# Four graph layers in one kernel: another place for the messages, squares as rows of the distance product, and new orders of the first two slots and of the last two graphs

## The reference

```
x = _layernorm(x + _L0(x, adj))
x = _layernorm(x + _L1(x, adj))
x = _layernorm(x + _L2(x, adj))
x = _layernorm(x + _L3(x, adj, nodemask))

# _L0: message passing with a gated state
h = relu(bn1(conv1(x.T)));  h = bn2(conv2(h, 17 taps));  x_conv = relu(h + x.T).T
s = x @ w_se.T + b_se                      # three columns
sq = sum(s * s, -1)
A = exp(-(sq[:, None] + sq[None, :] - 2 * s @ s.T)) * adj
x_nmp = A @ relu(x @ w_msg.T + b_msg)
r, z, n = gates of (x_conv, x_nmp, x);     return (1 - z) * n + z * x
# _L1: attention
X, q, k = leaky(x @ W_lin + b), leaky(x @ W_q), leaky(x @ W_k)
A = adj * sigmoid(q @ k.T * scale);  d = sum(A, -1) ** -0.5;  return (d * A * d) @ X
# _L2: hyperbolic aggregation
t = artanh(|x|) * x / |x|;  u = adj @ t;  return project(tanh(|u|) * u / |u|)
# _L3: normalised adjacency with its own loops
A = adj + I;  d = (sum(A, -1) + eps) ** -0.5;  return relu((d * A * d) @ (x @ W + b) * mask)
```

## Time and profile before

| what | us |
|---|---|
| median of the three runs shown | 773.96 |
| the profiled execution's own time | 773.77 |
| its span in the profile | 772.0 |
| PE busy | 709.7 (92%) |
| DVE busy | 625.5 (81%) |
| ACT busy | 423.6 (55%) |
| POOL busy | 138.0 (18%) |

### The profile page before, as it was taken

One profiled execution on the slowest core, in us unless ns is written; L12 is line 12 of the kernel. 1 busy time (PEld: TensorE's weight loads), 2 busy tenths in 40 slices (PEclk: granted clock), 3 DMA queues, 4 the chain that ended last, 5 costly groups with the idle time before them and its releaser, 6 DMA issues.

```text
span 772.0 us, 12824 instructions
## 1 busy us (share of the span) xinstructions
PE 709.7 (92%) x3984; PEld 547.4 (71%) x3984; DVE 625.5 (81%) x2080; ACT 423.6 (55%) x881; POOL 138.0 (18%) x151
## 2 busy tenths in 40 slices
PE   3879999999999999999999999999999999998553
PEld 1757877777787867777787867778687777775531
DVE  7456788888888888888888888888888888876655
ACT  4153754747374665748375665738465565734431
POOL 0000121221121111122121111112121121111221
PEclk9999999999999999999999999999999999998886
DMA  5304333150614233160513234060523324101000
GB/s 204 123 0 134 113 110 110 65 182 14 207 39 149 82 122 122 34 211 14 183 62 128 103 110 135 16 228 14 177 68 119 112 81 164 56 15 55 5 10 28
DMA packets 46585, 75.33 MB, mean 98 GB/s; under 512 B 4064, under 2 KB 12768, under 8 KB 46432
## 3 DMA queue, kind: packets, MB, share of 16 engines
q1 hardware_dynamic: 46560, 75.02, 28.9%
HBM read 70.82 MB, written 4.19 MB: 97 GB/s over the span
## 4 chain that ended last, share of the span: by engine, by line
PE 81%; ACT 10%; DVE 5%; issue 3%; POOL 1%; DMA 0%; SPq 0%; ACTq 0%; POOLq 0%; DVEq 0%
PE K L1267 11%; PE C L1395 7%; PE F L1403 7%; PE C L1327 7%; PE K L1432 7%; PE CONV L1300 6%; PE K L1300 6%; PE F L1327 6%; ACT JUNKD L487 5%; PE K L1260 4%; PE C L1267 3%; ACT A L454 3%; PE K L1381 2%; PE K L1287 2%; PE F L1383 2%
## 5 line engine op out<-in xcount | busy, mean ns | idle before, releaser
L337 POOL TENSOR_TENSOR RSTD<-VEPS,POW 128x4 f32<-128x4 f32 x48 | 48.9, 1019 | 276.7 <-DVE VEPS L687 276.7
L1300 PE MATMUL CONV<-H1H,WH 128*128 128x256 f32 x288 | 84.5, 293 | 0.0
L1300 PE MATMUL CONV<-H1L,WH 128*128 128x256 f32 x288 | 81.7, 284 | 0.0
L1300 PE MATMUL CONV<-H1H,WL 128*128 128x256 f32 x288 | 81.4, 283 | 0.0
L1395 PE MATMUL C<-QT,KT 128*128 128x512 f32 x128 | 62.0, 609 | 0.0
L1267 PEld LDWEIGHTS K<-XS,BIG 128*128 128x128 f32 x496 | 57.8, 192 | 1.3
L1267 PE MATMUL K<-XS,BIG 128*128 128x128 f32 x496 | 57.9, 275 | 0.0
L1403 PE MATMUL F<-A,MSG 128*128 128x512 f32 x128 | 57.6, 592 | 0.0
L1300 PEld LDWEIGHTS CONV<-H1L,WH 128*128 128x128 f32 x288 | 55.4, 192 | 0.6
L1300 PEld LDWEIGHTS CONV<-H1H,WH 128*128 128x128 f32 x288 | 55.3, 192 | 0.7
L1300 PEld LDWEIGHTS CONV<-H1H,WL 128*128 128x128 f32 x288 | 55.3, 192 | 0.0
(11 more groups left out here) (262 smaller groups left out, 1966.1 us busy)
## 6 DMA issues: line engine op xcount, KB each, us to landing
ADJF<-in_adjT SPq DMA_DIRECT2D x16, 1024.0 KB, 5.3
ADJN<-in_adj SPq DMA_DIRECT2D x16, 1024.0 KB, 7.6
ADJM<-in_adjT SPq DMA_DIRECT2D x15, 1024.0 KB, 5.6
ADJR<-in_adjT SPq DMA_DIRECT2D x14, 1024.0 KB, 5.2
X_IN<-in_xT SPq DMA_DIRECT2D x16, 256.0 KB, 2.6
out<-OUT SPq DMA_DIRECT2D x16, 256.0 KB, 2.7
BIG<-in_weights SPq DMA_DIRECT2D x1, 1088.0 KB, 5.2
BIG<-in_weights SPq DMA_DIRECT2D x1, 576.0 KB, 9.0
```

The costliest lines, as they stand in the source:

```text
L337: nc.gpsimd.tensor_tensor(RSTD[:, row, :], VEPS[:, row, :], POW[:, 0, :], ALU.pow).then_inc(ev[f"ln{layer}_rstd"], 1)
L1300: last = mm(out, w[:, at_col + k * P:at_col + (k + 1) * P], h[:, k:k + PH], start=(k == 0 and i == 0), stop=(k == count - 1 and i == 2))
```

## The change

Four things change.

1. In the repeating slot PE does `messages` no longer before `distances`, but after `first_norm_by_features`, which itself moves behind two odd taps; the projections follow.
2. `own_squares`, SQMAT and SQ go. The weights of `factors` now hold further copies of s in rows 32 to 43 of the product, b_se is added by a product of two rows (SEH by ONER, leading part and rest of b_se) at the head of `factors`, ACT squares rows 32 to 63 of K0 in place, and ZL, ZR, STL and STR take the squares as further rows of the distance product.
3. In slots 0 and 1 `first_taps` goes ahead of the transposes and distances; in the first, ACT makes two of the leading parts of the weights in place of DVE.
4. In the ending the orders of PE, ACT, DVE and POOL change: `attended(b)` ahead of `support(b)`, `support(c)` ahead of `last_aggregation(b)`, the second norm and the tangent of c ahead of the second residual of b, `last_sums(b)` behind c's degrees and norms. For this c takes other tiles (XRAW for X2, XX for Z3), PE's `support(c)` waits for z2 of b, DVE's last residual waits for a shift in place of ACT's output, and POOL waits for that output ahead of its last power.

The diff, cut to its core:

```diff
- SQ_BIAS, L_A, L_ZA, L_ZC, R_A, R_ZA, R_ZC) = range(21)
+ SE_LEFT, L_A, L_ZA, L_ZC, R_A, R_ZA, R_ZC) = range(21)
...
-        SQMAT = sb("SQMAT", [P, P])
+        SE = sb("SE", [2, P])
+        SEZ, SEH = sb("SEZ", [2, P], F32R), sb("SEH", [2, P], F32R)
+        ONER = sb("ONER", [2, N], F32R)
...
+        def summed_of(n):
+            return XX if n["last"] else Z3
+
+        def second_norm_of(n):
+            return XRAW if n["last"] else X2
...
-            sp.dma_start(SQMAT[:, :], sqmat_d).then_inc(s_const, 16)
+            sp.dma_start(SE[:, :], se_d).then_inc(s_const, 16)
...
                 shift(3, ROW[3], a["r"])
+                second_norm_powers(b["m"])
                 norm_power(b)
-                second_norm_powers(b["m"])
                 rstd(2, b["r"])
+                degree_power(c)
                 norm_power(c)
-                degree_power(c)
                 rstd(2, c["r"])
                 rstd(3, b["r"])
                 shift(3, ROW[3], b["r"])
+                pool.wait_ge(ev["out_ready"], every(b["r"]))
                 rstd(3, c["r"])
...
             def squares(count):
                 act.wait_ge(ev["g1_done"], count)
-                A(SQ[:, :], K0[:, :], ACT.Square, bias=PAR[:, SQ_BIAS:SQ_BIAS + 1]).then_inc(ev["sq_ready"], 1)
+                A(K0[SQUARES:2 * SQUARES, :], K0[SQUARES:2 * SQUARES, :], ACT.Square).then_inc(ev["sq_ready"], 1)
 
             def parts(count):
-                act.wait_ge(ev["g_done"], count)
+                act.wait_ge(ev["sq_ready"], count)
...
             parts(1)
+            act.wait_ge(s_conv2_w, 16)
+            A(WH[:, S_SUM:S_SUM + ODD * P], W[:, W_ODD:W_IH], ACT.Copy).then_inc(s_leading_act, 1)
+            act.wait_ge(s_rest_w, 16)
+            A(WH[:, S_IH:S_ALL], W[:, W_IH:W_SPLIT], ACT.Copy).then_inc(s_leading_act, 1)
...
             def second_norm(n):
-                act.wait_ge(ev["z2_ready"], every(n["r_prev"]))
-                norm_apply(1, lambda c: Z1[:, c, :], X2, n["r"], ev["x2_ready"])
+                if n["last"]:
+                    act.wait_ge(ev["xact_ready"], n["m"])
+                else:
+                    act.wait_ge(ev["z2_ready"], every(n["r_prev"]))
+                norm_apply(1, lambda c: Z1[:, c, :], second_norm_of(n), n["r"], ev["x2_ready"])
...
                 queries_and_keys(b)
                 linear(b)
                 act.wait_ge(ev["a1_23"], b["m_prev"])
-                sigmoids(b, 0, 2)
+                sigmoids(b, 0, C)
                 second_norm(b)
-                sigmoids(b, 2, C)
                 nc.scalar.preload_act_table_set("natural_log_exp_and_others")
                 artanh_log(b)
                 nc.scalar.preload_act_table_set("sigmoid_and_others")
                 support_norms(b)
+                second_norm(c)
                 support_tanh(b)
                 nc.scalar.preload_act_table_set("natural_log_exp_and_others")
-                output(16 * (b["r_prev"] - 1), b["r_prev"])
-
-                second_norm(c)
                 artanh_log(c)
                 nc.scalar.preload_act_table_set("sigmoid_and_others")
-                last_sums(b)
+                output(16 * (b["r_prev"] - 1), b["r_prev"])
                 degrees(c)
                 support_norms(c)
                 support_tanh(c)
+                last_sums(b)
                 last_sums(c)
                 output(16 * (c["r_prev"] - 1), c["r_prev"])
...
+            V.memset(ONER[:, :].bitcast(F32), 1.0)
             V.memset(H1L[:, :, :].bitcast(F32), 0.0).then_inc(s_set, 1)
...
-            def split(at_col, src, count):
+            def split(at_col, src, count, leading_of=None):
                 last = at_col + src.shape[1]
-                V.tensor_copy(WH[:, at_col:last], src).then_inc(s_leading, 1)
-                dve.wait_ge(s_leading, count)
+                if leading_of is None:
+                    V.tensor_copy(WH[:, at_col:last], src).then_inc(s_leading, 1)
+                    leading_of = s_leading
+                dve.wait_ge(leading_of, count)
                 return V.tensor_tensor(WL[:, at_col:last], src, WH[:, at_col:last].bitcast(F32), ALU.subtract)
...
+            V.tensor_scalar(SEZ[:, :], SE[:, :], PAR[0:2, SE_LEFT:SE_LEFT + 1], None, ALU.mult).then_inc(s_se, 1)
+            dve.wait_ge(s_se, 1)
+            V.tensor_tensor(SEH[:, :], SE[:, :], SEZ[:, :].bitcast(F32), ALU.subtract).then_inc(s_se, 1)
...
-            split(S_SUM, odd, 7).then_inc(s_split, 1)
+            split(S_SUM, odd, 1, s_leading_act).then_inc(s_split, 1)
...
-            split(S_IH, W[:, W_IH:W_SPLIT], 8).then_inc(s_split, 1)
+            split(S_IH, W[:, W_IH:W_SPLIT], 2, s_leading_act).then_inc(s_split, 1)
...
-            def tangent(n):
+            def tangent_factor(n):
...
+            def tangent_scaling(n):
                 dve.wait_ge(ev["f_ready"], n["r"])
                 dve.wait_ge(ev["x2_ready"], every(n["r"]))
                 dve.wait_ge(ev["agg2_done"], every(n["r_prev"]))
-                V.tensor_tensor(FX[:, :, :], X2[:, :, :], spread(T[:, 25, :]), ALU.mult).then_inc(
+                V.tensor_tensor(FX[:, :, :], second_norm_of(n)[:, :, :], spread(T[:, 25, :]), ALU.mult).then_inc(
                     ev["xt_ready"], 1)
+
+            def tangent(n):
+                tangent_factor(n)
+                tangent_scaling(n)
...
             def ending_residual(n):
-                dve.wait_ge(ev["out_ready"], every(n["r_prev"]))
+                if n["last"]:
+                    dve.wait_ge(ev["ln3_shift"], n["r_prev"])
+                else:
+                    dve.wait_ge(ev["out_ready"], every(n["r_prev"]))
...
-                tangent(b)
                 attention_degree(b)
+                tangent_factor(b)
+                scaled_attention(b)
+                tangent_scaling(b)
                 last_residual(a)
                 last_residual_stats(a)
-                scaled_attention(b)
-                norm_guard(b)
-                ball_factor(b)
                 first_residual(b, b["m"], b["m_prev"])
                 first_residual_stats(b["m"])
                 second_norm_moments(b["m"])
-                second_residual(b)
                 tangent_norm(c)
                 artanh_ratio(c)
+                norm_guard(b)
+                artanh_series(c)
+                tangent(c)
+                ball_factor(b)
+                second_residual(b)
                 own_loops(b)
                 scaled_norm(b)
-                artanh_series(c)
-                tangent(c)
                 third_norm(b)
...
+            pe.wait_ge(s_se, 2)
...
             def factors(count, previous):
                 pe.wait_ge(ev["xl"], count)
                 pe.wait_ge(ev["xconv_part"], previous)
-                product(K0[:, :], [(weight(W_SE), (XH[:, :], XL[:, :]))]).then_inc(ev["g1_done"], 1)
-
-            def own_squares(count):
-                pe.wait_ge(ev["sq_ready"], count)
-                mm(K0[:, :], SQMAT[:, :], SQ[:, :], start=False, stop=True, skip_group_check=True).then_inc(
-                    ev["g_done"], 1)
+                mm(K0[:, :], SEH[:, :], ONER[:, :], start=True, stop=False)
+                for k, (w, x) in enumerate(((WH, XH), (WH, XL), (WL, XH))):
+                    last = mm(K0[:, :], w[:, W_SE:W_SE + P], x[:, :], start=False, stop=(k == 2))
+                last.then_inc(ev["g1_done"], 1)
 
             first_conv(1, 0)
             factors(1, 0)
-            own_squares(1)
...
-                if not n["last"]:
+                if n["last"]:
+                    pe.wait_ge(ev["z2_ready"], every(n["r_prev"]))
+                else:
                     pe.wait_ge(ev["res_scaled"], n["r_prev"])
...
+                starting = isinstance(t, int) and t < 2
+                if starting:
+                    first_taps(n)
                 if mid:
                     state_by_nodes(n)
-                    messages(n)
                 distances(n)
-                if not mid:
-                    messages(n)
-                first_taps(n)
-                if mid:
-                    first_norm_by_features(n)
+                if not starting:
+                    first_taps(n)
                 even_taps(8, EVEN)
                 if n["first"]:
                     pe.wait_ge(s_split, 3)
                 odd_taps(0, 2)
+                if mid:
+                    first_norm_by_features(n)
+                messages(n)
                 if mid:
                     projections(n)
                 odd_taps(2, 8)
...
                     factors(n["f_next"], n["f"])
                     first_conv(n["f_next"], n["f"])
                 update_gate(n)
-                if following:
-                    own_squares(n["f_next"])
                 new_gate(n)
...
                 state_by_nodes(a)
-                messages(a)
                 distances(a)
                 first_taps(a)
-                first_norm_by_features(a)
                 even_taps(8, EVEN)
```

(58 more changed lines are left out.)

## The result

The kernel after takes 766.05 us (median of four runs, 764.36 to 766.93) against 774.52 us for the kernel before (four runs): a ratio of 0.9893, 95% interval 0.9872 to 0.9914. The forecast was 755.0, the range 749.5 to 762.0. The direction was right; of the 18.8 us of the sum some 8 came. The profiled execution took 766.93 us (span 765.1).

The account below looks back on a forecast made before the run. TensorE was taken as busiest, meeting VectorE's Y in a dead heat at the slot's end. First slot 6.1, second 1.8, steady slots 7.3, last full slot 0.6, ending 3.0: 18.8 us off 773.77 gives 755.0; range 749.5 to 762.

Parts of the forecast that it names:

- I take 0.234, the nearest: Head of the factors: the added two-row product costs 0.234 us, like an F32R pass; bounds 0.234 to 0.86.
- rival one: Two-row pass: an interruption on either side, twice 0.16 us for 14 graphs on Y's path, 4.5 us, giving 759.5; chance 0.27.
- The dead heat at the slot's end: Slot's end: PE's aggregation and DVE's Y end together, so none of PE's 0.63 us counts; PE waits about 0.7.
- The two just fit, so the 0.49 stays: Before the attention products: KT ends at 320.2, PE arrives at 320.28, so PE's gain of 0.49 us is kept.
- the slip of 0.17: DVE: message_sum waits for the messages until about 315.3, so everything behind it, to KT, slips by 0.17 us.
- 0.3 if KT is 0.3 late: Steady slot: lower bound of the messages' gain, 0.3 us in place of 0.64, if KT is 0.3 late.
- The 0.15 at the sigmoids: Attention products: ACT reaches its sigmoids about 0.5 us earlier, returning 0.15 of the 0.26 that PE lost there.
- the fifth rival: Steady slots: KT and message_sum slip by 0.5, slots keep 43.75 and only the ends gain, 763 us; chance 0.06.
- First slot: First slot: PE starts the aggregation at 26.0 instead of 32.12, gaining 6.1 us; bounds 4.5 to 6.4.
- the 1.9 forecast: Second slot: queries at 58.95 instead of 60.84, 1.9 us, less 0.08 at Y: 1.8; bounds 0.3 to 2.3.
- Ending: Last two graphs: earlier moments bring 1.5 to 2.4 us, the very end 0.8; 3.0 taken, bounds 0 to 4.2.

Follow-up runs that it names:

- all three edits: Kernel after with bias product on 128 rows, STR behind Y plus three taps before the distances, QT and KT ahead of the artanh series: 748.25 us, ratio 0.9657.

## Why the prediction was right and wrong

**The two-row pass: the step that failed most.** The step "I take 0.234, the nearest" was short by 0.38: the pass and its two changes cost 0.62 in place of 0.234. It stood where the prediction said it would, on Y's path, so Y came 0.34 late in every slot in place of 0.08. The mechanism is rival one, written as 2 x 0.16 and measured as 0.38; it got a chance of 0.27 because no row showed such a product. The nearest row was near in type and width, not in rows, and rows decided. The squares alone cost 0.0076 x 774 = 5.9 us, where the sum charged 13 x 0.08 = 1.0.

**The dead heat at the slot's end: right, its size by luck.** PE waits 0.61 for Y (forecast about 0.7), none of its saved time counts, and the squares alone are slower. But the 0.61 is made up otherwise: PE saved 0.86 - 0.62 = 0.24 in place of 0.63, and Y came 0.34 late in place of 0.08.

**Queries and KT: the wait moved.** The wait of 0.55 at the queries is gone, as forecast. The step "The two just fit, so the 0.49 stays" failed. KT ends 11.76 after Y (359.19 - 347.43), before 11.67: the slip of 0.17 was even generous. But the products start 0.28 after KT's end (359.47), not at it, and the step had left 0.08. From Y's end to the end of the attention products it was 320.77 + 3.70 - 308.36 = 16.11 and is 359.47 + 3.79 - 347.43 = 15.83: a gain of 0.28, where 0.64 was forecast. This was written as a bound ("0.3 if KT is 0.3 late") and not taken. Why 0.28 us pass between KT's end and the products is open; Y's transposes start 0.05 after Y's end.

**The 0.15 at the sigmoids: mostly wrong.** From the start of the first attention product to the start of the products behind them (layer 2's) it is 363.09 - 359.47 = 3.62 after, 324.31 - 320.61 = 3.70 before by the same timeline. Earlier work of ACT gave back 0.08 at most.

Together in a slot: 0.28 from the messages, -0.34 from the squares, and the slot stays at 43.755 (the one that is read here is 43.78 long, its counterpart before 43.73). That is the outcome of the fifth rival, but not its cause: it had KT 0.5 late, and KT was 0.09 late; it did not have the two-row product.

**First slot: right to the aggregation, then lost.** The first aggregation starts at 26.36, 5.8 ahead of the chain of the earlier trace rows and 5.6 ahead of the timeline (forecast 6.1). The first taps ran at half speed as forecast, 0.21 us apart until 19.1, where the same taps are 0.12 apart in a later slot. (The two casts that DVE lost were taken as 0.62 and 0.75; in the kernel before the subtractions follow them by 0.72 and 0.79.) By Y's transposes only 52.55 - 48.92 = 3.6 is left; first before, then after, then the run with the ending undone:

```profile
31.96 3.60 PE L1403 MATMUL F<-A,MSG 128*128 128x512 f32 x8
```

```profile
26.36 3.67 PE L1437 MATMUL F<-A,MSG 128*128 128x512 f32 x8 [1.12 <-issue]
...
48.92 0.66 PE L1384 MATMUL F<-IDENT,Y 128*128 128x128 f32 x4 [1.33 <-DVE Y L790]
```

```profile
26.65 3.67 PE L1417 MATMUL F<-A,MSG 128*128 128x512 f32 x8 [1.11 <-issue]
...
47.64 0.66 PE L1366 MATMUL F<-IDENT,Y 128*128 128x128 f32 x4 [0.78 <-DVE Y L782]
```

The two are 22.56 apart in after; with the ending undone, with the same instructions there and a full clock, 47.64 - 26.65 = 20.99; before, 52.55 - 31.96 = 20.59. So the low clock cost 1.6 in this execution, the slowest of the four, and the other 0.4 is the two-row product: with 128 rows it is 20.61. The prediction had looked for a low clock at the first taps and at the waits of the second slot, not behind the first aggregation. The second slot itself gave 1.5 of the 1.9 forecast from Y's end to the attention (13.07 to 11.56 by the two chains): Y's transposes ran at full clock (0.66).

**Ending: right in size.** 3.0 was forecast, 3.6 with the last full slot; the pair of traces shows 2.45 with that slot, the run that undoes the ending 3.6 to 4.4 without it. The attended products of the last graph start 717.77 - 700.20 = 17.57 after its queries, where it was 726.41 - 704.75 = 21.66: 4.1 earlier, as forecast, and their first half ran at half speed, as forecast. First before, then after:

```profile
704.75 2.08 PE L1381 MATMUL CONV<-X1T,WF 128*128 128x512 f32 x2 [0.69 <-ACT X1T L481]
...
726.41 1.95 PE L1267 MATMUL K<-XS,BIG 128*128 128x128 f32 x16
```

```profile
700.20 2.08 PE L1415 MATMUL CONV<-X1T,WF 128*128 128x512 f32 x2 [0.69 <-ACT X1T L500]
...
717.77 3.78 PE L1301 MATMUL K<-XS,BIG 128*128 128x128 f32 x16 [2.46 <-DVE XS L998]
```

**Range.** It reached to 762; the first rival, with every other term kept, gave 759.5. Here three terms fell together: the two-row pass, KT, and the clock of the first slot. The chain of a slot runs through both places, from Y over KT and the attention to the factors, H1H and the next Y, so a gain of 0.3 at one and a loss of 0.3 at the other leave nothing; and the upper end of a range has to add up the bounds, not take one rival at a time.

## What to carry to other kernels

In a loop whose iteration ends in a dead heat between two engines, cost each path on its own and to the start of the consumer, not to the end of the producer: 0.28 us after KT's end took some 0.2 of a forecast gain of 0.49. A product of few rows amid products of 128 can be dearer than one padded with zeros; where it stands on the path, pad it (to 96 or 128 rows here), or put several narrow ones of one shape side by side. When a change brings less than its parts, run its parts alone: here one of four lost 5.9 us, and with that, a late KT and STR's place mended the same change gives 3.4% in place of 1.1%.

## What the runs showed of the hardware that was not expected

A product over 2 or 64 rows between products of 128 rows (F32R, 512 columns) costs 0.38 us more than with 96 or 128 rows, and the loads on either side of the change start 0.23 later against their products; the second of two such products in a row adds 0.24, a plain pass. And the granted clock after one and the same wait of 1.33 us, in one and the same order of instructions, was 0.50 in one execution and 1.00 in another, worth 1.6 us. With the bias product on 128 rows the granted clock showed no fall behind the first aggregation; with all three edits it came later, 0.57 on average from 52 to 56 us, and so it did with KT earlier and with STR behind Y (0.50 from 54 to 56). At the very start the granted clock of the profile says little: it reads 1.00 from 16 to 18 us, where the taps ran at half speed. What decides where it falls was not settled: no run here tells it apart.
